# A decoder layer on one core: the long filter's second half laced with the first inverse and Gram products, values first in the last group, the gate's input loaded earlier

## What is computed

```python
A = where(strict_lo, kb @ k.T, 0)                 # Gram product, decay by beta
Tinv = solve_triangular(eye + A, eye)             # inverse of a unit lower triangle
u, w = Tinv @ v, Tinv @ kb
S = S + k_i.T @ (u_i - w_i @ S)                   # scanned over the chunks
short, long_ = fir(v, fir_short_w), fir(v, fir_long_w)   # causal, 3 and 31 taps
gate_in = concat([hs, short.mean(2), long_.mean(2), delta.mean(2)])
wgt = softmax(gelu(gate_in @ fg_w1.T + fg_b1) @ fg_w2.T + fg_b2, temperature)
o = wgt0 * short + wgt1 * long_ + wgt2 * delta + wgt3 * v    # then RMS norm, output projection
```

## Time and profile before

| | |
|---|---|
| runs | 1143.61, 1147.48, 1141.53 us (median 1143.61) |
| the profiled execution | 1144.12 us, its span 1142.30 us |
| busy in the span | PE 87%, DVE 70%, POOL 55%, ACT 46% |
| granted clock of PE, mean | 0.95 |
| start of group 0's solves | 245.23 us |
| end of group 0's gate hidden layer | 274.04 us |

### The profile page before, as it was taken

One profiled execution on the slowest core, in us unless ns is written; L12 is line 12 of the kernel. 1 busy time (PEld: TensorE's weight loads), 2 busy tenths in 40 slices (PEclk: granted clock), 3 DMA queues, 4 the chain that ended last, 5 costly groups with the idle time before them and its releaser, 6 DMA issues.

```text
span 1142.3 us, 26147 instructions
## 1 busy us (share of the span) xinstructions
PE 997.4 (87%) x9538; PEld 733.1 (64%) x9538; DVE 803.6 (70%) x2110; ACT 528.2 (46%) x992; POOL 622.9 (55%) x1009
## 2 busy tenths in 40 slices
PE   4899997887699899899999989989989999988991
PEld 2465657765476676576666667667667667767891
DVE  2879984543676866787677687687678775657487
ACT  2877774513333532542443443353253255755770
POOL 5469898438126636816816735653673215335562
PEclk9999998869799989999989999999999999999996
DMA  9444534450101250260161152122111173224589
GB/s 197 133 163 143 175 93 149 151 157 19 57 20 42 75 151 21 65 185 31 65 183 38 47 141 93 48 70 77 38 55 58 56 266 110 90 89 128 166 286 341
DMA packets 87100, 127.69 MB, mean 112 GB/s; under 512 B 28352, under 2 KB 62784, under 8 KB 84800
## 3 DMA queue, kind: packets, MB, share of 16 engines
q1 hardware_dynamic: 79776, 106.30, 30.2%
q0 software_dynamic: 7200, 19.74, 4.8%
HBM read 66.47 MB, written 59.55 MB: 110 GB/s over the span
## 4 chain that ended last, share of the span: by engine, by line
PE 45%; POOL 20%; DVE 20%; issue 8%; ACT 4%; DMA 1%; SPq 1%; ACTq 0%; DVEq 0%; POOLq 0%
POOL arena L1544 7%; POOL arena L1546 7%; DVE arena L1673 3%; PE bank L562 3%; PE bank L499 3%; PE bank L734 3%; PE bank L468 2%; PE bank L970 2%; POOL orn L1562 2%; PE bank L816 2%; POOL arena L1434 2%; PE bank L576 2%; PE bank L436 2%; PE bank L934 2%; PE bank L588 2%
## 5 line engine op out<-in xcount | busy, mean ns | idle before, releaser
L1044 ACT ACTIVATE arena<-bank 128x512 f32<-128x512 f32 (+4 forms) x358 | 185.9, 539 | 348.8 <-PE bank L961 61.8
L1544 POOL TENSOR_TENSOR arena<-arena 128x126 f32<-128x126 f32 (+22 forms) x248 | 107.0, 432 | 43.9 <-DVE arena L1732 26.1
L1673 DVE SCALAR_TENSOR_TENSOR arena<-arena,param 128x512 f32<-128x512 f32 x144 | 104.1, 777 | 18.8 <-ACT arena L1067 18.1
L1607 POOL DMA_INDIRECT results<-arena x78 | 76.3, 978 | 71.2 <-DVE arena L2225 42.9
L1546 POOL TENSOR_TENSOR arena<-arena 128x126 f32<-128x126 f32 (+22 forms) x248 | 102.2, 412 | 19.4
L419 PE MATMUL bank<-const,arena 128*128 128x128 f32 x256 | 40.5, 310 | 52.7 <-DVE arena L2162 26.7
L1489 POOL DMA_INDIRECT slots_x<-arena x64 | 63.6, 994 | 37.3 <-DVE arena L1964 21.4
L970 PE MATMUL bank<-arena 128*128 128x128 f32 x624 | 83.6, 277 | 0.2 <-ACT arena L1344 0.2
L1513 POOL TENSOR_TENSOR arena<-arena,rb 128x256 f32<-128x256 f32 x32 | 19.7, 616 | 116.5 <-ACT arena L1044 116.0
L970 PEld LDWEIGHTS bank<-arena 128*128 128x128 f32 x624 | 76.9, 194 | 0.4 <-issue 0.4
L1442 POOL COPY arena<-arena 32x128 f32<-32x128 f32 x128 | 53.5, 418 | 38.2 <-DVE arena L1722 31.4
(11 more groups left out here) (293 smaller groups left out, 2635.6 us busy)
## 6 DMA issues: line engine op xcount, KB each, us to landing
arena<-slots_x SPq DMA_DIRECT2D x78, 129.0 KB, 2.1
slots_x<-rows_of_no_token SPq DMA_DIRECT2D x8, 1161.0 KB, 11.7
xt<-x_in SPq DMA_DIRECT2D x16, 512.0 KB, 5.6
kq<-kq_T SPq DMA_DIRECT2D x8, 1024.0 KB, 9.0
arena<-results SPq DMA_DIRECT2D x32, 256.0 KB, 4.8
kq_T<-kq SPq DMA_DIRECT2D x7, 1024.0 KB, 3.9
arena<-ffn_in SPq DMA_DIRECT2D x7, 768.0 KB, 4.1
vT<-v_T SPq DMA_DIRECT2D x8, 514.0 KB, 4.0
```

Source lines behind the costliest of these rows:

```text
L1044: free(act.activation(out_, in_, func, **kw), name)
L1544: own.link(pool.tensor_tensor(tmp, rows32[:, m0:, k].unsqueeze(2).broadcast_to([P, nm, k]), units[:, 0:k, k].unsqueeze(1).broadcast_to([P, ...
L1607: pool.indirect_dma_start(results[:, :], bass.IndirectOffsetOnAxis(ap=dest[:, n % YS:n % YS + 1], axis=0), ys[:, n % YS, :], None).then_in ...
L1673: ins = V.scalar_tensor_tensor(cv[:, k % 4, :], pre[:, j, d:d + GT], param[:, at:at + 1], cv[:, k % 4, :], ALU.mult, ALU.add)
```

## The change

- In the last group the chunks come in the order key 0, value 0, value 1, key 1, query 0, query 1; `spread(7)` stands on DVE after the fifth chunk's second tap, ahead of its last; SP stores that group's values before its keys. All six chunk loops go by position `k`, the buffers and counters with it.
- SP issues five taps' loads per group, not four. It loads the gate's input `load_hs(0)` right behind `load_v(0)`, ahead of the long filter's stores. `load_long(0)` and the two `load_rows` come ahead of the fills of no-token rows, which no longer wait for POOL's tables.
- PE: `square_sums(7)` moves from before the filters to behind `long_filter(0, 3)`. Group 0's inverse and values are laced with filters `(1, 0)` to `(1, 3)`, and `next_gram(1, t)` with `(1, 4)` to `(1, 7)`. The filter uses three banks (4, 5, 6), not six.
- ACT follows this order. It empties all four solves of group 0 and waits only for the first half's turns to do so.
- DVE clears `Tf` (POOL did), turns the first half, makes the scales, then group 1's Gram parts and units, all before `body(0)`. The second half's turns stand in `body(0)`: two before the tile products and six behind them; one tap of the short filter stands behind each of the first three outputs.
- `longS[1]` moves into the space of the first half's spread values, `outer` of group 0 into `kvt[1]`.
- POOL runs group 1's elimination before `body(0)`, then its tables; in `body(0)` it does the output norm first, then `front_rows(1)`.
- `head_means` of group 0 moves behind the loop over tiles, the gate's product with it. `front_values(1, t)` moves from the loop over tiles to the end of group 0, on PE behind the output projection, on ACT behind `front_blocks(1)`.

```diff
-        longS = [lead[:, c * 4096:(c + 1) * 4096].rearrange("p (n k) -> p n k", k=QB) for c in range(CK)]
+        longS = [arena[:, a_:a_ + 4096].rearrange("p (n k) -> p n k", k=QB) for a_ in (0, LATE)]
...
+        def chunks(i):
+
+            return (0, 4, 5, 1, 2, 3) if i == NG - 1 else tuple(range(6))
...
-            long_bank = cycle((0, 1, 2, 4, 5, 6))
+            long_bank = cycle((4, 5, 6))
...
                 for t in range(T):
-                    if ahead:
+                    if x and ahead:
                         front_values(i + 1, t)
...
                 if x:
                     values_turned(3)
+                else:
+                    head_means()
                 gate_hidden(1, 0)
...
                     if ahead and k == 0:
                         pair_inner(i + 1)
+                if not x:
+                    for t in range(T):
+                        front_values(1, t)
...
-            for t in range(T):
-                long_filter(0, t)
-            for t in range(T):
-                long_filter(0, 4 + t)
-            for t in range(T):
-                long_filter(1, t)
-                front_values(0, t)
-            for t in range(T):
+            for k in range(8):
+                long_filter(0, k)
+                if k == 3:
+                    square_sums(NG - 1)
+            pair_inner(0)
+            long_filter(1, 0)
+            front_values(0, 0)
+            pair_corner(0)
+            long_filter(1, 1)
+            front_values(0, 1)
+            half_inner(0)
+            long_filter(1, 2)
+            front_values(0, 2)
+            half_corner(0)
+            long_filter(1, 3)
+            front_values(0, 3)
+            keys_loaded(1)
+            for t in range(T):
+                next_gram(1, t)
                 long_filter(1, 4 + t)
...
+            pair_inner(0)
+            long_filter(1, 0)
+            front_values(0, 0)
             act.wait_ge(setup_main, N_MAIN_SETUP)
             front_blocks(0)
+            pair_corner(0)
+            long_filter(1, 1)
...
                 if i == 0:
-                    front_solve(1)
-                    front_steps(1)
+                    output_norm()
                     front_rows(1)
...
             front_rows(0)
-            drained(pool, "long07")
-            pool.memset(Tf, 0.0).then_inc(setup_main, 1)
+            front_solve(1)
+            front_steps(1)
             pool.wait_ge(sem("long_ready"), CK * NG)
             tile_tables()
...
+                    if k == 4 and i == NG - 1:
+                        spread(i)
...
                 else:
-                    filled(dve, f"outer1.{i}")
-                    for t in range(T):
-                        front_gram(1, t)
-                    solved_rows()
-                    front_units(1)
+                    long_turned(1, range(2))
...
+                if not x:
+                    long_turned(1, range(2, NG))
+                    dve.wait_ge(sem("long_ready"), CK * NG)
...
                     outputs(t)
+                    if not x and t < FS:
+                        short_filter((t,))
...
             front_second(0)
+            drained(dve, "long07")
+            V.memset(Tf, 0.0).then_inc(setup_main, 1)
+            long_turned(0, range(NG))
             later_scales()
-            for c in range(CK):
-                long_turned(c)
+            filled(dve, "outer1.0")
+            for t in range(T):
+                front_gram(1, t)
+            filled(dve, "edge1.0")
+            front_units(1)
...
-                for q in range(4 * i, 4 * i + 4):
+                for q in range(5 * i, min(5 * i + 5, QB)):
                     load_taps(q)
...
+                if i < NG - 1:
+                    store_kq()
+                    store_v()
+                else:
+                    store_v()
+                    store_kq()
...
             load_v(0)
+            sp.wait_ge(sem("hs_stored"), 16 * NG)
+            sp.wait_ge(sem("beta_done"), NG - 1)
+            load_hs(0)
```

More of the change, by code:

```diff
@@ L818, in gate_hidden, with head_means @@
                         full(last, n)
[L820 to L823, removed]
-                for c in range(CK):
-                    mm(o[0:DH, :], cst("mean_s")[:, 0:DH], sht[:, c, :], start=c == 0, stop=c == CK - 1)
-                    last = mm(o[DH:2 * DH, :], cst("mean_l")[:, DH:2 * DH], lng[:, c, :], start=c == 0, stop=c == CK - 1)
-                full(last, n)
+                def head_means():
+                    n = f"gm.{i}"
+                    o = open_bank(pe, n, next(body_bank))
+                    pe.wait_ge(sem("short_done"), 2 * i + 2)
+                    pe.wait_ge(sem("long_loaded"), 16 * (i + 1))
+                    for c in range(CK):
+                        mm(o[0:DH, :], cst("mean_s")[:, 0:DH], sht[:, c, :], start=c == 0, stop=c == CK - 1)
+                        last = mm(o[DH:2 * DH, :], cst("mean_l")[:, DH:2 * DH], lng[:, c, :], start=c == 0,
+                                  stop=c == CK - 1)
+                    full(last, n)
+                if x:
+                    head_means()
                 if x and ahead:
@@ L1094, in _ @@
             for i in range(NG):
-                for j in range(3):
-                    project(i, j)
+                for k in range(3):
+                    project(i, k)
                 if i:
@@ L1103, in _, with last_stat @@
                         .then_inc(sem("tanh_ready"), 1)
[L1104 to L1108, removed]
-                        hidden_rows(i + 1)
[L1110 to L1117, removed]
+                for k in range(3):
+                    silu(i, k)
+                    square(i, k)
+                    project(i, 3 + k)
+                    if k == 1 and i + 1 < NG:
+                        hidden_rows(i + 1)
+                for k in range(3, 6):
+                    silu(i, k)
+                    square(i, k)
+            def last_stat():
+                stat(NG - 1)
+                drained(act, f"stat.{NG - 1}")
+                act.activation(beta[:, 1:NG, :, :], st[:, 1:NG, :, 8:12], ACT.Tanh, scale=0.5)\
+                    .then_inc(sem("tanh_ready"), 1)
             def long_filter(c, k):
@@ L1223, in solved_rows @@
             def solved_rows(i):
-                for t in range(T // 2):
+                for t in range(T // 2 if i else T):
                     n = f"solve{t}.{i}"
@@ L1583, in body @@
                     norm_scale(1, "x", 2 * x + 2)
-                if not (i and ahead):
+                if i and not ahead:
                     output_norm()
@@ L1759, in _ @@
                     halo(i + 1)
-            spread(NG - 1)
             def later_scales():
@@ L1765, in later_scales, with long_turned @@
                 scales(slice(1, NG))
-            def long_turned(c):
+            def long_turned(c, groups):
                 for k in range(8):
                     drained(dve, f"long{c}{k}")
-                for i in range(NG):
+                for i in groups:
                     k = NG * c + i
```

161 lines of the change are left out of this document (83 added, 78 removed).

## The result

The changed kernel takes 1135.92 us (median of 11 runs, 1132.13 to 1143.84) against 1143.58 us (11 runs) before: ratio 0.9935, interval 0.9915 to 0.9956. That is 7.7 us or 0.67% less, just over the 0.5% that a measurement can tell. The forecast was 1136.5. The profiled execution's span fell from 1142.30 to 1134.0 us. Lines are those of the changed kernel from here on, if nothing else is said.

What follows compares the result with a forecast made beforehand. No engine alone was taken to bound the kernel; waits from 164 to 304 us did. Terms -13.5 + 0.4 + 1.7 - 3.35 + 6.8 + 0.8 = -7.15 from 1144.12 gave 1137.0, as median 1136.5; range 1129 to 1145.

Steps and rivals of the forecast that it cites:

- step 4: Group 0's solves to the gate's hidden layer: +0.4 us for VectorE's added work, +1.7 for a clock fall after bank waits.
- step 6: Start of group 1: values' transposes between output projection and corner product add 6.8 us, a further clock fall 0.8.
- Step 1: Last group: values come earlier, 12 taps instead of 16 precede their transposes; filters start at 176.9 instead of 180.91 us.
- Step 2: First half's filters, with square sums behind the fourth and 2.59 + 1.25 us kept for the burst; inverse starts at 199.7.
- S: The start of group 0's inverse, behind the first half's filters; forecast at 199.7 us.
- The rival without a stall: No stall in the transfer burst: inverse starts at 195.9, 3.85 us sooner, total 1132.7, or 1129 if clock holds; chance 0.20.
- Step 3: Laced stretch, inverse start to group 0's solves: 32.0 us, bounds 30 and 36, solves at 231.7, 13.5 us earlier.
- Step 5: VectorE's blend: GpSimd's output norm first removes a 3.819 us multiply-add; -3.35 us, bounds -3.35 and 0.
- Edits at zero: Gate's input sooner, five taps a group, later no-token fills and group 1's later value load: each expected to cost nothing.
- The second rival: Given back, no change: TensorE held until the burst ends (+4), clock falls twice more (+2 to 3); 1142 to 1143; chance 0.21.
- The slower rival: Clock stays at half through the laced stretch: 1153.5 us, slower than before once about 13 us run at half speed; chance 0.07.

Runs made afterwards that it cites:

- the old order: Changed kernel with the last group's chunks, its values' transposes and two stores back in their old places: 1140.96 us, ratio to before 0.9978.
- the unlaced kernel: Changed kernel with second-half filters and values, group 0's inverse and group 1's Gram products again one behind the other: 1149.80 us, ratio 1.0047.
- GpSimd's order alone: Kernel before, with GpSimd doing group 0's output norm ahead of its row scalings: 1140.69 us, ratio 0.9973.
- the early values: Changed kernel with group 1's value transposes moved into TensorE's wait for the normed output: 1129.44 us, ratio 0.9873; again 1128.12 us, 0.9855.
- both edits: Changed kernel with group 1's values earlier and VectorE's first output product ahead of the last two turns: 1121.65 us, 0.9806; again 1122.39 us, 0.9817.
- VectorE's first product earlier: Changed kernel with VectorE's first output product of group 0 ahead of the second half's last two turns: 1134.44 us, ratio 0.9915.

## Why the prediction was right

The forecast was 0.6 us over the median, closer than its terms were: the solves came 2.75 us sooner than forecast, and step 4 and the clock behind step 6 gave 1.9 of that back. That the two errors cancel is luck.

*Step 1* (filters at 176.9) measured 175.76, of which 0.76 is the taps' own earlier start, 163.91 for 164.67; shown by the old order, in which the filters start 3.8 us later and the end comes 4.9 later.

*Step 2* failed: S = 199.7 was forecast, 196.0 measured, 1.1 of it by step 1. The term "2.59 + 1.25" was kept because the burst remained, and it came as 0.52 with no fall of the clock; in the seven other traces with the values first it did not come at all. The rival without a stall had S right to 0.1, in part by luck: it has 19.0 us from the filters' start to S, 20.3 were measured, and the earlier start made that up. The kernel before with the square sums behind the fourth filter has 0.64 us left of the wait, so their place accounts for most of it. What TensorE waits for is its next 256 instructions, the refill which the Trainium skill describes (Runtime: NRT & Kernel Launch, Instruction fetch mechanics). Its "mostly hidden" agrees with the 0.52 us after and not with the 2.59 before.

*Step 3* had 32.0 for the laced stretch, measured 33.0; the half-speed filter at 207 (3.52 us instead of 1.95) is the difference, and the five laced traces without it have 30.9 to 31.7. Solves 16.25 sooner instead of 13.5: 1.1 by step 1, 2.6 by step 2, less 1.0 here. The unlaced kernel gives the lacing 12.5 to 13.9 us at the solves.

*Step 4* had +2.1, measured +3.4. What it added 1.7 for (a wait for a shared bank, then half the clock) came, and was under-sized: half speed lasted from 244.3 to 254.6, and with the wait closed and the clock held the stretch takes 28.6 us, 3.7 less. In the laced kernels the fall goes with the wait (all four traces that have it, none of the three with it closed, up to 249 us); the unlaced kernel shows that it needs something more. VectorE, which step 4 had carry the stretch, did not carry it to its end; it was done at 253.2, and TensorE's half-speed products set the end.

*Step 5* had -3.35, measured -3.6 in the change, and alone -3.1 (trace and ratio) to -3.65 (medians). By the lock of one instruction that the Trainium skill states (SBUF — State Buffer, SBUF: two separate sides) it would have been 0.6; the measurement decides, and here one operation of 3.8 us lasted about as long as the six scalings of 0.60 us in a row beside it. The run with GpSimd's order alone, where the engines took turns (1.09 and 1.07 us), agrees with that rule.

*Step 6* had +6.8, measured +6.7, and the early values give 6.5 of it back. Its +0.8 for the clock and whatever else follows came as +1.4, of which 1.2 lie between the corner product and group 1's solves.

*Edits at zero*: none shows as a wait in the change as it stands, but only two were undone, and together. The gate's input was no free edit. It carries step 4's new order, and without it (and with four taps) the change loses 11 to 13 us and ends slower than before. The cover named, "the whole inverse", holds for the early load only.

The second rival (1142 to 1143) had one of its parts, the clock falling twice in the body and the laced stretch; its other part, TensorE held until the burst ended, did not come. The slower rival needed 13 us at half speed in the laced stretch, and 3.5 came.

## What to carry to other kernels

A chain of small dependent products is cheapest between bulk products of the same engine: here that was worth 12.8 us at the end by the ratios, 13.9 by the medians, in idle time and in clock. Ask of every group of instructions that a change moves away whether the wait it now stands in front of is longer than itself; the values of the next group cost 6.7 us in front of an inverse and nothing in the 12 us wait just ahead. An edit that costs nothing may be what another edit stands on, so cost it with the others in place. An engine that loads nothing can still wait in a burst of transfers, since its instructions come by DMA too; where a wait is for nothing on record, count the instructions ahead of it.

## What was not expected

TensorE's refill of instructions showed at all, as 2.0 to 2.6 us in the kernel before, and as most of the short waits in the laced stretch.

Gains at two places may not add. Closing the bank's wait alone brought 1.5 us by the medians, behind the early values 5.7. The traces give a reason, group 1's half clock behind the first, but the noise of the medians leaves open how much it is worth.

The granted clock did not follow the wait ahead of it alone. Behind the same 1.29 us wait for the bank it fell after the change (0.53 from 244 to 255) and stayed at 1.00 in the unlaced kernel. The filter at 207 ran at half speed after the change and in both traces with both edits, and at full speed in the early values' two and in that with VectorE's first product earlier, with waits of 0.2 to 0.7 us ahead of it in all; TensorE's instructions are the same up to there in these six. So the order of the program does not decide it, and what does was not settled.

One VectorE operation on two operands in SBUF took 3.8 us instead of 0.5 beside GpSimd's row scalings, another, beside the first of them, 0.4 us more than without, and the transposes beside the rest no more.
